# Head outputs of a 12-head attention as four column groups of TensorE, with the softmax sums taken from the exponentials

## What is computed

```python
qkv = x @ w_qkv.T
q, k, v = jnp.split(qkv, 3, axis=-1)
q, k, v = map(to_heads, (q, k, v))          # B, 12, N, 16
q = _rope(q * scale)
k = _rope(k)
attn = jnp.einsum('bhid,bhjd->bhij', q, k)
attn = jax.nn.softmax(attn, axis=-1)
out = jnp.einsum('bhij,bhjd->bhid', attn, v)
out = out.transpose(0, 2, 1, 3).reshape(B, N, C)
return out @ w_proj.T + b_proj
```

## Time and profile before

| | us |
|---|---|
| median of 3 runs | 1556.29 (1554.89 to 1559.04) |
| the profiled execution, whole time | 1558.22 |
| its span, first to last instruction | 1556.5 |
| mean granted TensorE clock over the span | 0.934 |
| the stage: first mix on PE to the last counts | 938.96 to 1392.3 |

### The profile page before, as it was taken

The page is one execution under the profiler, slowest core; times in us unless marked ns, Lnnn a source line. Parts: engine busy times, 40 slices in busy tenths (PEclk is TensorE's granted clock), DMA queues, the critical chain, the costliest instruction groups (busy, mean ns, idle before and its releaser), DMA issues. The chain is left out here.

```text
span 1556.5 us, 28510 instructions
## 1 busy us (share of the span) xinstructions
PE 1431.4 (92%) x8824; PEld 1269.1 (82%) x8824; DVE 978.6 (63%) x2877; ACT 891.0 (57%) x1833; POOL 270.8 (17%) x255
## 2 busy tenths in 40 slices
PE   3899999985899999999999986999999999957995
PEld 1577777774799999999999976999999999956985
DVE  6776666442777777777777744777776777632231
ACT  1377777774666666666666642655555555524551
POOL 5411100000111111111111101122121212120434
PEclk9999999998899999999999997889898989867998
DMA  7035655576466666666666654434333436105542
GB/s 198 25 123 146 146 135 135 140 172 149 136 200 186 193 189 196 187 190 197 189 189 190 199 155 148 129 108 126 114 125 99 121 116 190 31 11 148 134 91 20
DMA packets 202698, 220.87 MB, mean 142 GB/s; under 512 B 30065, under 2 KB 169528, under 8 KB 202606
## 3 DMA queue, kind: packets, MB, share of 16 engines
q1 hardware_dynamic: 170254, 179.96, 41.5%
q10 hardware_dynamic: 24672, 32.79, 6.2%
q0 software_dynamic: 7680, 6.95, 2.4%
HBM read 142.27 MB, written 79.90 MB: 143 GB/s over the span
## 5 line engine op out<-in xcount | busy, mean ns | idle before, releaser
L1062 PE MATMUL bank<-e_w,e_h_full 128*128 128x192 f32 x1920 | 324.5, 326 | 0.3
L1062 PEld LDWEIGHTS bank<-e_w,e_h_full 128*128 128x128 f32 x1920 | 310.6, 190 | 1.2 <-ACT e_h_full L1123 0.8
L1123 ACT ACTIVATE e_h_full<-bank,e_b 128x512 f32<-128x512 f32 x240 | 165.1, 689 | 196.7 <-PE bank L60 196.7
L1000 POOL TENSOR_TENSOR e_ln_rstd<-e_ln_var_eps,minus_half 128x4 f32<-128x4 f32 x64 | 64.8, 1013 | 524.2 <-DVE e_ln_var_eps L1173 524.2
L1180 DVE TENSOR_SCALAR e_rows<-e_slot_sums,e_ln_mean_var,e_ln_rstd 128x192 f32<-128x192 f32 x256 | 79.9, 376 | 76.2 <-POOL e_ln_rstd L1000 76.2
L1096 ACT ACTIVATE e_x_full<-bank,e_ln_shift,e_ln_gain 128x512 f32<-128x512 f32 x128 | 92.6, 773 | 53.3 <-PE bank L1035 48.5
L585 DVE TENSOR_REDUCE column_neg_max<-bank 128x4 f32<-128x512 f32 x64 | 44.3, 692 | 115.1 <-PE bank L60 103.7
L1351 POOL TENSOR_TENSOR ln_rstd<-ln_var_eps,minus_half 128x2 f32<-128x2 f32 (+1 forms) x35 | 51.8, 1481 | 345.5 <-DVE ln_var_eps L1652 345.5
L60 PE MATMUL bank<-e_x_hi,e_w1hi 128*128 128x512 f32 x240 | 105.4, 439 | 5.3 <-DVE e_w1lo L1159 3.5
L830 PE MATMUL bank<-x,dispatch_weights 128*128 128x193 f32 x512 | 97.0, 333 | 14.1 <-ACT slot_stage L690 13.5
L1412 PE MATMUL bank<-slot_out_and_one,combineT 128*128 128x193 f32 x512 | 94.5, 338 | 10.9 <-DMA slot_out_and_one<-slot_outputs 10.9
(11 more groups left out here) (214 smaller groups left out, 3071.5 us busy)
## 6 DMA issues: line engine op xcount, KB each, us to landing
slot_sums<-slot_stage SPq DMA_DIRECT2D x64, 386.0 KB
e_slot_sums<-slot_sums SPq DMA_DIRECT2D x64, 386.0 KB, 3.6
slot_outputs<-e_stage ACTq DMA_DIRECT2D x64, 384.0 KB, 3.4
slot_out_and_one<-slot_outputs SPq DMA_DIRECT2D x32, 768.0 KB
e_w<-in_w SPq DMA_DIRECT2D x64, 288.0 KB, 3.0
slot_logits<-kept_logits SPq DMA_DIRECT2D x64, 256.0 KB
slot_logits<-slot_logits SPq DMA_DIRECT2D x32, 512.0 KB, 3.4
e_w1raw<-in_w SPq DMA_DIRECT2D x80, 192.0 KB, 2.7
```

The source lines that it names most:

```text
L1000: pool.tensor_tensor(rs[u][:], ve[u][:], half[:], ALU.pow).then_inc(rstd_ready, 1)
L1062: last = pe.matmul(ybank(u)[:, j // 2, (j % 2) * D:(j % 2 + 1) * D], hf[:, k, js], w2s[u][:, k, :], start=k == 0, stop=k == MT - 1)
L1123: act.activation(hf[:, m, :], hbank(u, m), act_fn, bias=b1s[:, m, ds(n, 1)]).then_inc(acted, 1)
```

## The change

Seven things change in the stage; their order in the code matters as much as their content.

1. The head outputs take v as the weight (128 rows, 32 columns: 16 of v and 16 more, of which one is 1 for head 0 and the others are 0) and the transposed probabilities as the moving side (128 columns). The four heads s of a group g write to PSUM partitions 32 s to 32 s + 31, so each uses another group of 32 columns of TensorE. The result is already turned.
2. The sums come from `accum_out` of the exponentials on ACT. DVE inverts 128 x 12 of them, spreads them to 128 x 384, PE turns that with three transposes, ACT copies it, and DVE multiplies it into the head outputs (`oT`) at the start of the next turn. The two transposes of the outputs, ACT's two copies, and DVE's old reciprocal and multiplication are gone.
3. The projection has three weights of 128 rows with zero padding, and the bias stands in one of their rows: three matmuls instead of two.
4. On PE the mix Y of y goes to the front of the turn, ahead of the product of q and the projection of p, and the head outputs go from the middle of the turn to its end, behind S.
5. On DVE the statistics of the layer norm behind Y come ahead of the rotation, x4 right behind it, the residual and statistics of p next, then the inversion, and less_max, `place` or `choose` last. POOL takes two square roots of one column a turn instead of one of two columns.
6. The four row maxima become two of 128 x 768.
7. The router's weights and the count's operands are padded to 128 columns. The router's two loads go from SP's queue in an earlier stage to ACT's queue at the start of this stage, behind two clears on DVE.

```diff
-        self.Wp0, self.Wp1 = sb("Wproj0", [P, D]), sb("Wproj1", [DR + 1, D])
-        self.rw0, self.rw1 = sb("router0", [P, NE1]), sb("router1", [P, NE1])
+        self.Wp = sb("Wproj_padded", [P, 3, D])
...
-        sp.dma_start(self.Wp0[:], ins["Wproj"][0:P]).then_inc(self.tables_in, 16)
-        sp.dma_start(self.Wp1[:], ins["Wproj"][P:D + 1]).then_inc(self.tables_in, 16)
-        sp.dma_start(self.rw0[:], ins["router"][0:P]).then_inc(self.router_in, 16)
-        sp.dma_start(self.rw1[DR:P, :], ins["router"][P:D]).then_inc(self.router_in, 16)
+        sp.dma_start(self.Wp[:], ins["Wproj"]).then_inc(self.tables_in, 16)
...
-        vs = [sb(f"v_and_one{u}", [P, NH, HD + 1]) for u in range(2)]
+        vs = [sb(f"v_padded{u}", [P, NH, 2 * HD]) for u in range(2)]
...
-        oinv, o = sb("head_inv", [P, NH]), sb("attn_out", [P, D])
-        oT0, oT1 = sb("oT0", [P, P]), sb("oT1", [DR + 1, P])
+        esum, einv = sb("head_exp_sum", [P, 4, 3]), sb("head_inv", [P, 4, 3])
+        einv_wide, oT = sb("head_inv_wide", [P, 3, 4, 2 * HD]), sb("oT", [P, 3 * P])
+        einvT = sb("head_invT", [P, 3 * P])
...
+        rw0, rw1 = sb("router0", [P, P]), sb("router1", [P, P])
...
-        heads = bank[:, 3, D:D + NH * (HD + 1)].rearrange("p (a d) -> p a d", d=HD + 1)
+        head_out, head_inv = bank[:, 1, 0:3 * P], bank[:, 2, 0:3 * P]
...
-                def rsqrt(t, y, p):
-                    c = slice(0 if y is not None else 1, 2 if p is not None else 1)
-                    pool.wait_ge(S["ln_var"], t + 1)
-                    pool.tensor_tensor(rs[:, c], ve[:, c], half[:, c], ALU.pow).then_inc(S["ln_rstd"], 1)
+                def rsqrt(k, n):
+                    pool.wait_ge(S[f"ln{k + 4}_var"], n + 1)
+                    pool.tensor_tensor(rs[:, k:k + 1], ve[:, k:k + 1], half[:, 0:1], ALU.pow
+                                       ).then_inc(S[f"ln{k + 4}_rstd"], 1)
...
+                    if y is not None:
+                        if y == 0:
+                            pe.wait_ge(S["ones_set"], 4)
+                        pe.wait_ge(ys_in[u], 16 * (y // 2 + 1))
+                        pe.wait_ge(S["C_exp"], y + 1)
+
+                        past(pe, S["h2_ready"], y)
+                        past(pe, S["x4_split"], y)
+                        for c in range(NC):
+                            last = pe.matmul(bank[:, 0, 0:D + 1], cT[:, c, :], ysb[u][:, c, :],
+                                             start=c == 0, stop=c == NC - 1)
+                        last.then_inc(S["Y_done"], 1)
...
-                        past(pe, S["o_ready"], q - 1)
+                        past(pe, S["einvT_took"], q - 1)
+                        past(pe, S["v_took"], q)
...
-                        pe.wait_ge(S["oT_took"], 2 * p + 2)
-                        matmuls(pe, projected, [(oT0[:], Wp0[:]), (oT1[:], Wp1[:])]).then_inc(S["p_done"], 1)
...
+                        pe.wait_ge(S["o_ready"], p + 1)
+                        matmuls(pe, projected, [(oT[:, g * P:(g + 1) * P], Wp[:, g, :]) for g in range(3)]
+                                ).then_inc(S["p_done"], 1)
...
-                        matmuls(pe, bank[:, 7, 0:2 * NE1], [
-                            (upto[:], onehot[:].rearrange("p j e -> p (j e)")),
-                            (ones[:], so_far[:].rearrange("p j e -> p (j e)"))]).then_inc(S["counted"], 1)
+                        matmuls(pe, bank[:, 7, 0:P], [(upto[:], onehot_wide[:]), (ones[:], so_far_wide[:])]
+                                ).then_inc(S["counted"], 1)
...
-                            last = matmuls(pe, bank[:, 7, j * NE1:(j + 1) * NE1],
+                            last = matmuls(pe, bank[:, 7, j * P:(j + 1) * P],
...
-                    if a is not None:
-
-                        pe.wait_ge(S["v_took"], min(a + 2, NB))
-                        for k in range(3):
-                            pe.wait_ge(S["pT_took"], 3 * a + k + 1)
-                            for m in range(4):
-                                s, g = divmod(k * 4 + m, 3)
-                                hd = 4 * g + s
-                                last = pe.matmul(heads[:, hd, :], pT[:, s, g, :], vs[u][:, hd, :],
-                                                 start=True, stop=True)
-                        last.then_inc(S["g_done"], 1)
...
-                        pe.wait_ge(S["o_ready"], a + 1)
-
-                        past(pe, S["h3_ready"], a)
-                        pe.transpose(bank[:, 1, 0:P], o[:, 0:P], ident[:])
-                        pe.transpose(bank[0:DR, 1, P:2 * P], o[:, P:D], ident[:]).then_inc(S["oT_done"], 1)
+                        past(pe, S["qk_took"], min(t, NB))
+                        pe.wait_ge(S["einv_ready"], a + 1)
+                        for g in range(3):
+                            last = pe.transpose(bank[:, 2, g * P:(g + 1) * P],
+                                                einv_wide[:, g, :, :].rearrange("p s d -> p (s d)"), ident[:])
+                        last.then_inc(S["einvT_done"], 1)
+                        pe.wait_ge(S["pT_took"], 3 * a + 3)
+                        pe.wait_ge(S["v_took"], a + 1)
+
+                        past(pe, S["h3_ready"], t - 2)
+                        for g in range(3):
+                            for s in range(4):
+                                last = pe.matmul(bank[32 * s:32 * s + 32, 1, g * P:(g + 1) * P], vs[u][:, 4 * g + s, :],
+                                                 pT[:, s, g, :], start=True, stop=True)
+                        last.then_inc(S["head_out_done"], 1)
...
-                    if p is not None:
-                        act.wait_ge(S["oT_done"], p + 1)
-                        act.activation(oT0[:], bank[:, 1, 0:P], ACT.Copy).then_inc(S["oT_took"], 1)
-                        act.activation(oT1[0:DR, :], bank[0:DR, 1, P:2 * P], ACT.Copy).then_inc(S["oT_took"], 1)
                     if a is not None:
                         for s in range(4):
-                            act.wait_ge(S["head_max"], 4 * a + s + 1)
+                            act.wait_ge(S["head_max"], 2 * a + s // 2 + 1)
+                            past(act, S["einv_ready"], a)
                             for g in range(3):
                                 last = act.activation(pr[:, s, g, :], bank[:, 4 + s, g * P:(g + 1) * P], ACT.Exp,
-                                                      bias=nmx[:, s, g:g + 1])
+                                                      bias=nmx[:, s, g:g + 1], accum_out=esum[:, s, g:g + 1])
                             last.then_inc(S["S_exp"], 1)
                     if q is not None:
                         if q == 0:
-                            act.wait_ge(S["ones_set"], 5)
...
+                        act.wait_ge(S["einvT_done"], a + 1)
+                        past(act, S["o_ready"], a)
+                        act.activation(einvT[:], head_inv, ACT.Copy).then_inc(S["einvT_took"], 1)
...
+                act.wait_ge(S["router_cleared"], 1)
+                act.dma_start(rw0[:, 0:NE1], ins["router"][0:P]).then_inc(router_in, 16)
+                act.dma_start(rw1[DR:P, 0:NE1], ins["router"][P:D]).then_inc(router_in, 16)
...
                     if a is not None:
                         past(dve, S["S_exp"], 4 * a)
-                        for s in range(4):
-                            dve.wait_ge(S["S_done"], 4 * a + s + 1)
-                            dve.tensor_reduce(nmx[:, s, :], group4(bank[:, 4 + s, :])[:, 0:3], AX_X, ALU.max,
+                        for k in range(2):
+                            dve.wait_ge(S["S_done"], 4 * a + 2 * k + 2)
+                            dve.tensor_reduce(nmx[:, 2 * k:2 * k + 2, :], bank[:, 4 + 2 * k:6 + 2 * k, 0:3 * P]
+                                              .rearrange("p s (g n) -> p s g n", g=3), AX_X, ALU.max,
                                               negate=True).then_inc(S["head_max"], 1)
+                    if p is not None:
+
+                        dve.wait_ge(S["head_out_done"], p + 1)
+                        past(dve, S["p_done"], p)
+                        dve.wait_ge(S["einvT_took"], p + 1)
+                        dve.tensor_tensor(oT[:], head_out, einvT[:], ALU.mult).then_inc(S["o_ready"], 1)
...
+                        dve.wait_ge(S["S_exp"], 4 * a + 4)
+                        past(dve, S["einvT_done"], a)
+                        st.link(dve.reciprocal(einv[:], esum[:]))
+                        dve.tensor_copy(einv_wide[:], einv[:].rearrange("p s g -> p g s").unsqueeze(3)
...
-                        dve.wait_ge(S["g_done"], a + 1)
-                        st.link(dve.reciprocal(oinv[:], heads[:, :, HD]))
-                        past(dve, S["oT_done"], a)
-                        dve.tensor_tensor(o[:].rearrange("p (a d) -> p a d", d=HD), heads[:, :, 0:HD],
-                                          oinv[:].unsqueeze(2).broadcast_to([P, NH, HD]), ALU.mult
-                                          ).then_inc(S["o_ready"], 1)
```

136 lines of the change are left out of this document (72 added, 64 removed).

## The result

| | before | changed |
|---|---|---|
| median, same chip | 1557.64 us (1554.89 to 1559.04) | 1544.31 us (1541.98 to 1546.11) |
| the profiled execution, whole time | 1558.22 us | 1546.11 us |
| its span | 1556.5 us | 1544.4 us |
| 32 mixes on PE, first start to last | 410.5 us | 391.2 us |
| granted clock between 1000 and 1300 us | 0.89 | 0.97 |

The changed kernel is faster: 0.9916 of the time of before, 95% interval 0.9893 to 0.9938, where the forecast of 1538 us stood for 0.988 of its own base of 1556.29. Of all the executions behind this document one, of e_off_ring (1553.34 us), fell in a slower state of the chip, and medians and intervals leave it out. Two profiled executions differ by 12.1 us in all, and by 19.3 us in the stage.

A forecast was written before the change was run, and what follows sets the result against it. PE bounded the old kernel; the changed one would be bound by a closed ring through DVE: 12.3 + 0.25 us of clock dips = 12.55 against 13.2, 19.5 us over 30 turns off 1558.2, stated as 1538 us, range 1520 to 1572.

The forecast's parts named there:

- The ring: Closed chain from mix over DVE's row, bank 7's read, scores, transposes and head outputs to the next mix; 12.3 us.
- Its items: The steps of one even turn at full clock, each counted in full, summing to 12.3 us; odd turns 12.2.
- nearest row: Head outputs on PE: no row shows column groups, so the scores' row groups stand in; 0.85 us for 24 passes.
- Rival B: Head outputs on PE: column groups do not overlap, outputs stay at 2.6 us, ring 14.05, time 1583 us; chance 0.15.
- The exponentials: ACT: accum_out adds a second instruction, repeat 0.39 us against 0.26, 1.6 us more, hidden in a second ring of 11.
- D: A third step (exponentials, POOL's square root or a slower inverse copy) joins the ring: turn 12.95, 1550 to 1551; chance 0.13.
- the square root: x4's square root on POOL: 1.46 us, hidden beside the rotation's 1.60 by a tenth; longer than that would add.
- No stretch of narrow streams is left: PE's clock: only PE's waits remain to lower it; the stage's clock should be above 0.95.
- C: Groups overlap but the clock falls as often, behind PE's waits ahead of the scores: 1567 us; chance 0.12.
- the dips that are left: Clock falls now and then from PE's waits ahead of the scores: 0.25 us a turn allowed of the 1.8.
- The sum: 12.55 us a turn against 13.2, 0.65 for each of 30 turns: 19.5 us off 1558.2, said as 1538.
- Zero: Stage start: clears and router's loads of 3 to 4 us fit DVE's 8.62 us wait for the first mix; no cost.

The follow-up runs named there:

- e_off_ring: e_slots_ahead with bank 7 read before the inversion, the split of x4T right behind it, and the rest of place and choose, x5, less_max later; 1532.94 us.
- e_mix_back: The changed kernel with the mix back in its old place on PE, behind the product of q and the projection of p; 1656.94 us.
- e_slots_ahead: The changed kernel with less_max done one turn ahead on DVE, behind place and choose; 1519.87 us.
- e_same_columns: The changed kernel with head outputs reordered so that three neighbours in a row use the same 32 columns of TensorE; 1578.85 us.
- the second profile: The changed kernel profiled once more, with nothing altered; 32 mixes in 390.8 us, median 1545.06 us.
- e_before_wide: The kernel before with its head outputs streaming 128 columns in place of 17 past the same weights; 1524.39 us.
- e_narrow_streams: The changed kernel with the router's product streaming 8 columns and the counts 16 again, past the same weights; 1583.49 us.
- e_maxima_first: e_slots_ahead with the two row maxima right behind the split of x4T, x5 and less_max after, and ACT copying x4T before the mixing weights' exponentials; 1508.40 us.

## Why the prediction was right, and where its size was off

- **Bound and mechanism.** Right. The ring through mix, DVE's row, bank 7, scores and head outputs is the turn: at full clock 12.26 us in an odd turn and 12.33 in an even one, where 12.2 and 12.3 were forecast. With clock dips the mean of 31 turns is (391.2 - 2.5) / 31 = 12.54 against 12.55. e_mix_back and e_slots_ahead lengthen and shorten it, at full clock by 2.6 and 0.47 us. PE's wait is ahead of the scores and for DVE, as forecast, 38.0 us in 300 or 1.6 a turn.
- **Its items.** Mix to DVE 2.93 (forecast 2.99), scale and statistics 1.48 (1.47), rotation 1.59 (1.60), x4 0.51 (0.52), residual and statistics of p 1.21 (1.22), less_max 1.14 (1.22), `choose` and the hop to PE 0.49 (0.50), scores 0.91 (0.87), transposes 0.48 (0.42), head outputs 0.79 (0.85). Too low was only the inversion, 0.73 for 0.60, since its copy takes 0.55 and not 0.44. The small errors of the others cancel it.
- **Column groups.** Right as a nearest row, and for the reason given (e_same_columns). Rival B is out.
- **The exponentials.** A repeat of 0.34 us (1210.56 to 1210.90), not 0.39, and off the ring; D did not come about. Nor did it for the square root, forecast 1.46 us, which took 0.56. The reading behind the forecast was wrong: in the earlier trace rows the 1.46 us lie beside DVE's less_max (956.67 to 957.89), and of the six square roots of 128 x 1 in the kernel before the three beside a less_max take 1.44 to 1.46, the three others 0.54 to 0.58. Item 5 took less_max away from there.
- **The clock.** "No stretch of narrow streams is left" was the right reading, C is out, and the window runs at 0.97. The price of the dips that are left was too low: the 25 full turns take 12.70 us in the mean, 0.40 above the ring at full clock, where 0.25 were allowed. The shorter turns of the fill, 11.87 us, hide that in the mean of 31, so that 12.54 meets 12.55 is in part luck. It did not hurt the sum, since the kernel before had shorter turns there too: 0.61 us less in each full turn and 0.72 in each of the first six, where 0.65 was forecast. But I priced item 7 at nothing, as padding that costs nothing, and never asked what leaving it out would cost. It carries the change: 34.7 us of 32 mixes hang on it. And I put the clock's part at up to 1.8 us a turn and then let the ring take it: 13.2 - 1.8 = 11.4 us would have said that a kernel which takes the clock alone beats the forecast turn of 12.55, and I didn't draw it. It does, by 23 us in the stage (e_before_wide).
- **The sum.** 30 x 0.65 = 19.5 us for the stage: 19.3 measured, 19.7 in the second profile. What was off is the step behind it, from the stage to the whole: the sum was taken from the one profiled execution of before, which was one with a quick first part, and a forecast of a difference from one execution inherits all that moves in it. The changed kernel's own profile had 8.6 us of that part against it. Two slips in the sum are smaller: 1538.7 less the 1.9 us that it names is 1536.8 and not 1538, and B's 1583 and C's 1567 leave the 1.9 out. Over 12 and 17 runs on another chip the medians are 1545.06 and 1562.3, 17 us apart.
- **Start, fill and drain.** "Zero": PE waits 10.9 us for the first slot outputs in either kernel, and the drain differs by 1.4 us. Right, though the clears and the router's loads took 7.1 us (942.87 to 949.95) and not 3 to 4; DVE's first read of the mix comes at 952.5.

## What to carry to other kernels

When weights set the pace of a product, stream as many columns as the pace gives free: it cost nothing here and was worth more than a new algorithm for the same product. Many narrow passes brought the clock down in a PE that never waited (24 of 17 columns a turn, 0.89), a few only where PE waited as well (e_narrow_streams, 0.88, against e_before_wide, 1.00). Before shortening an engine, close the ring: write down who waits for whom until you are back at the start, and do it for every ring that shares an engine, since an order that shortens one lengthens the other (e_off_ring lost 36 us against e_maxima_first). Before work goes to POOL, look at what DVE does at that moment: 1.1 us taken off DVE came back as 1.8 us on a product of 16 elements. Price a ring by its turns at full clock, and the clock apart from it. And read a difference from the stage it was made in: whole times here carried up to 19 us of something else.
